# A fused attention and expert block with a deeper ring of gelus and a new hand-written order of its turn

## The reference

```python
h = tok(x); h = concat([h, txt], axis=1)                 # (64, 193, 128)
h = h + attn(layernorm(h))
h = h + ffn(layernorm(h))

# attn: 8 heads of 16; q and k have 8 features each, v has 16
qkv = group_norm(x @ W_qkv)                              # 32 groups, over tokens and features
logits = q k^T + q . rpe_k[i - j] + k . rpe_q[i - j]     # relative positions
attn = softmax(logits)
out = attn v + attn . rpe_v[i - j]
return group_norm(out)

# ffn: 8 experts of 512 hidden features, all of them computed, with the two top gate probabilities
for i in range(2):
    w_in = x * top_p[i]                                  # normalised to sum 1
    h = gelu(w_in @ W1 + b1)                             # exact gelu
    out += h @ W2 (summed over the experts) + sum(b2)
```

## Time and profile before

| | |
|---|---|
| median of 3 runs | 3409.49 us (3407.18 to 3465.08) |
| profiled execution | 3410.88 us, span 3409.1 us |
| mean granted TensorE clock | 0.987 |
| busy | PE 3132.8 us (92%), PEld 2577.5, ACT 1912.9 (56%), DVE 1897.9 (56%), POOL 1421.7 (42%) |
| first stage, start and the turn with attention alone | up to about 345 us |
| then | turns of 97.8 us |

### The profile page before, as it was taken

One profiled execution on the slowest core, in us unless ns is written; L12 is line 12 of the kernel. 1 busy time (PEld: TensorE's weight loads), 2 busy tenths in 40 slices (PEclk: granted clock), 3 DMA queues, 4 the chain that ended last, 5 costly groups with the idle time before them and its releaser, 6 DMA issues.

```text
span 3409.1 us, 62207 instructions
## 1 busy us (share of the span) xinstructions
PE 3132.8 (92%) x20032; PEld 2577.5 (76%) x20032; DVE 1897.9 (56%) x4113; ACT 1912.9 (56%) x4370; POOL 1421.7 (42%) x1350
## 2 busy tenths in 40 slices
PE   6977999999999999999999999999999999999998
PEld 5866778777777777777777777777777777777776
DVE  4644555555555555555555555555555555555554
ACT  4632555665555556655555566555555665555556
POOL 1001444454434444544344454444444544444446
PEclk9987999999999999999999999999999999999999
DMA  9951110111111001111110011111100111111010
GB/s 203 221 168 42 25 26 5 26 26 25 25 24 26 22 9 26 26 25 25 24 26 16 15 26 26 24 26 24 26 9 22 26 26 24 26 24 26 4 23 5
DMA packets 92173, 121.51 MB, mean 36 GB/s; under 512 B 8414, under 2 KB 86558, under 8 KB 87710
## 3 DMA queue, kind: packets, MB, share of 16 engines
q1 hardware_dynamic: 87714, 118.24, 14.9%
q10 hardware_dynamic: 4432, 2.93, 0.4%
HBM read 106.17 MB, written 14.97 MB: 36 GB/s over the span
## 4 chain that ended last, share of the span: by engine, by line
PE 54%; POOL 15%; issue 15%; DVE 5%; ACT 3%; POOLq 0%; DMA 0%; ACTq 0%; SPq 0%; DVEq 0%
POOL gelu L892 14%; PE bank L518 8%; PE bank L519 8%; PE bank L421 7%; PE bank L563 5%; PE bank L564 5%; PE bank L531 5%; PE bank L545 3%; PE bank L430 3%; PE bank L434 2%; PE bank L431 2%; PE bank L573 2%; PE bank L494 1%; PE bank L462 1%; ACT gelu L819 1%
## 5 line engine op out<-in xcount | busy, mean ns | idle before, releaser
L892 POOL TENSOR_TENSOR gelu<-gelu 128x386 f32<-128x386 f32 x1024 | 1040.3, 1031 | 1034.9 <-ACT gelu L820 1034.6
L819 ACT ACTIVATE gelu<-bank,b_s 128x386 f32<-128x386 f32 x1024 | 596.1, 582 | 805.2 <-DVE gelu L609 783.5
L421 PE MATMUL bank<-gelu,w_s 128*128 128x386 f32 x2048 | 842.0, 498 | 82.7 <-POOL gelu L892 82.7
L609 DVE TENSOR_TENSOR gelu<-bank,ratio 128x386 f32<-128x386 f32 x1024 | 565.8, 556 | 518.0 <-PE bank L434 514.6
L820 ACT ACTIVATE gelu<-gelu,b_s 128x386 f32<-128x386 f32 x1024 | 623.9, 609 | 0.0
L430 PE MATMUL bank<-x_hi,w_hi 128*128 128x386 f32 x1024 | 555.3, 542 | 73.5 <-ACT gelu L819 69.2
L421 PEld LDWEIGHTS bank<-gelu,w_s 128*128 128x128 f32 x2048 | 366.3, 191 | 149.5 <-POOL gelu L892 132.9
L860 ACT ACTIVATE lp<-bank,mx 128x193 f32<-128x193 f32 x800 | 328.9, 418 | 170.6 <-DVE mx L712 170.2
L518 PE MATMUL bank<-k_f,q_bd 128*128 128x193 f32 x1600 | 396.7, 330 | 8.4 <-DVE a_bd L702 8.4
L519 PE MATMUL bank<-rw,a_bd 128*128 128x193 f32 x1600 | 393.8, 328 | 0.0
L430 PEld LDWEIGHTS bank<-x_hi,w_hi 128*128 128x128 f32 x1024 | 194.7, 190 | 239.5 <-ACT gelu L819 140.3
(11 more groups left out here) (132 smaller groups left out, 4343.6 us busy)
## 6 DMA issues: line engine op xcount, KB each, us to landing
a_rep<-u_scratch SPq DMA_DIRECT2D x32, 1600.0 KB, 9.8
xt<-in_x SPq DMA_DIRECT2D x192, 196.0 KB
txt_s<-in_txt SPq DMA_DIRECT2D x32, 128.0 KB, 2.1
u_scratch<-k_f SPq DMA_DIRECT2D x32, 100.0 KB, 2.2
u_scratch<-q_f SPq DMA_DIRECT2D x32, 100.0 KB, 2.2
out<-o_s SPq DMA_DIRECT2D x64, 48.5 KB
out<-o_s SPq DMA_DIRECT2D x64, 48.0 KB
rv<-in_rel_v SPq DMA_DIRECT2D x1, 2624.0 KB, 14.6
```

The lines of the kernel that those rows point to most:

```text
L421: mm(yb[:, 0:T2], w2_s[:, f, :], gelu1[:, f % RING, :], start=(f == 0), stop=(f == NF - 1)).then_inc(S["w2_done"], 1)
L609: v.tensor_tensor(gelu2[:, f % RING, :], zb[f % 2][:, 0:T2], ratio[:, :], ALU.mult).then_inc(S["z2_done"], 1)
L819: a(gelu1[:, f % RING, :], zb[f % 2][:, 0:T2], ACT.Gelu, bias=b1_s[:, f:f + 1]).then_inc(S["g_done"], 1)
L892: g.tensor_tensor(gelu1[:, f % RING, :], gelu1[:, f % RING, :], gelu2[:, f % RING, :], ALU.add).then_inc(S["hs_done"], 1)
```

## The change

The ring has eight slots instead of four, and W2 runs four steps behind W1 instead of three; so there are four w2t at the end of a turn, and the first W2 of a pair comes with its fifth W1. The semaphores hs_done and w2_done start at RING, so that the waits for a slot need no special case. The norm copies of gaff on ACT are two steps of their own, nqk (q and k) and nv (v), and ACT's part of oaff is the step onorm. And the string has a new order. The work is the same.

```diff
-RING = 4
-LAG = 3
+RING = 8
+LAG = 4
-EARLY = "txt mean1 var1 bc1 proj gmean gvar gaff".split()
+EARLY = "txt mean1 var1 bc1 proj gmean gvar gaff nqk nv".split()
 SCHEDULE = (
-    "c c c am0 c qs0 c c vt hkeep log0 am1 log1 qs1 log2 am2 log3 qs2 log4 log5 am3 log6 qs3 log7 txt log8 "
-    "qs4 log9 mean1 log10 log11 var1 log12 tr0 tr1 bc1 rel0 c tr2 inv rel1 c tr3 rel2 tr4 rel3 tr5 rel4 tr6 rel5 rel6 "
-    "proj c pv0 c rec0 gmean pv1 c rec1 gvar place0 c place1 gaff c c omean c ovar c c oaff c oh2 c mean2 c var2 c c "
-    "bc2 c gate c c gate2 c c c c bcast w2t xin w2t w2t ot a otr a ocopy hres a"
+    "c qs0 vt am0 qs1 c c hkeep log0 am1 am2 log1 log2 txt log3 log4 mean1 log5 am3 log6 log7 log8 qs2 log9 log10 qs3 log11 qs4 log12 c var1 c tr0 c c inv tr1 rel0 tr2 rel1 tr3 rel2 tr4 bc1 rel3 c tr5 rel4 tr6 c rel5 rel6 proj pv0 gmean rec0 pv1 rec1 gvar place0 place1 c omean c gaff ovar c c c c c nqk c c oaff c onorm c oh2 c c mean2 nv c c var2 c c bc2 c gate gate2 c c bcast w2t w2t xin w2t w2t ot a a otr hres a ocopy"
...
         def ring_wait(eng, sem_, f, n):
-            if f >= RING or not is_first(n):
-                eng.wait_ge(sem_, n * NF + f - RING + 1)
+            eng.wait_ge(sem_, n * NF + f + 1)
...
-                pe.wait_ge(S["hs_done"], n * NF + f + 1)
+                pe.wait_ge(S["hs_done"], n * NF + f + 1 + RING)
...
-                    dve.wait_ge(S["w2_done"], n * NF + NF)
+                    dve.wait_ge(S["w2_done"], n * NF + NF + RING)
...
+            dve.sem_inc(S["hs_done"], RING)
+            dve.sem_inc(S["w2_done"], RING)
...
-                if s == "gaff":
+                sc, bi = gst[:, 5, :], gst[:, 6, :]
+                if s == "nqk":
                     act.wait_ge(S["affine"], t + 1)
-                    sc, bi = gst[:, 5, :], gst[:, 6, :]
                     for k, dst in enumerate((q_f, k_f)):
                         a(dst[:, 0:L], misc[:, 256 * k:256 * k + L], ACT.Identity,
                           bias=bi[:, k:k + 1], scale=sc[:, k:k + 1]).then_inc(S["norm"], 1)
+                elif s == "nv":
                     for b in range(2):
                         a(e2[:, b * L:(b + 1) * L], lg[0][:, b * L:(b + 1) * L], ACT.Identity,
                           bias=bi[:, 2 + b:3 + b], scale=sc[:, 2 + b:3 + b]).then_inc(S["norm"], 1)
...
-                elif s == "oaff":
+                elif s == "onorm":
                     act.wait_ge(S["oaffine"], t + 1)
```

## The result

The changed kernel took 3210.81 us (median of 4 runs, 3208.32 to 3213.52), beside 3408.34 us for the kernel before: a ratio of 0.9422, interval 0.9404 to 0.9441. The forecast was 3225 us, its range 3163 to 3315. The gain is 197.5 us, 6.4 us for each of the 31 turns.

A forecast was written before the change was run, and what follows sets the result against it. PE bounds each 97.80 us turn, with waits costing 9.5 us; remaining terms of 2.7, times 1.28, make 3.5, so 6.0 us gained over 31 turns: 3410.9 − 186 = 3225 us, range 3163 to 3315 (8 in 10).

The forecast's parts named there:

- Lag: At W2: the extra step removes five waits for POOL's sums, saving 4.05 us per turn; 0.15 remains at the last W2.
- Norm copies: W1 behind ACT's norm copies: loss falls from 1.83 to 0.35 us per turn, the v copies costing nothing.
- onorm and mean2: Output norm: two steps cover mean2's 1.34 us wait for oh2; onorm on ACT delays a W1 by 0.47 us.
- Start of the turn: Four W1 without a W2 instead of three: third to fifth W1 late by 0.53, 0.46 and 0.11, together 1.1 us.
- the factor 1.28: On the summed remaining waits: allowance for error in the step-by-step timing, raising 2.7 to 3.5 us per turn.
- Gate: Before the broadcast: gate2 follows gate with no product between, a 2.5 us chain; PE waits about 0.4 us.
- Attention part: Attention steps: moved products cover the transposes' wait; the remainder falls from 1.0 to 0.2 us per turn.
- SP: a_rep's load after later q/k copies: lands at t + 24, needed at t + 36.7; no wait, 12.7 us to spare.
- rival C: am0 holds DVE and every product until a_rep lands; slower, 3480 us in all; chance 0.04.
- Rival A: gaff, oaff, am0 and x_lo on DVE each wait for a POOL instruction: 2.9 us per turn, 3315 us; chance 0.15.
- Rival B: At the gate, POOL reaches the pow three sums behind; DVE and broadcast wait 2.9 us, 3315 us; chance 0.08.
- Rival D: W2's waits are ended by ACT's pace, not POOL's order: 4.05 us stay, 3350 us; no separate chance given.

The follow-up runs named there:

- e_new_small: The changed kernel's new step order with four slots and W2 three steps behind W1, instead of eight and four: 3331.7 us, ratio 0.9772.
- e_r8l3: The changed kernel with its eight slots and new order, but W2 three steps behind W1 instead of four: 3333.7 us, ratio 0.9781.
- e_joined: The changed kernel with the four norm copies together again, right behind gaff: 3250.1 us, ratio 0.9536.
- e_split_old: The kernel before with only the norm copies taken apart, q and k behind omean, v behind mean2: 3367.8 us, ratio 0.988.
- e_better2: The changed kernel with POOL's first two q spreads in the turn before, mean1 one logit later, a product between gate and gate2: 3158.0 us.
- e_ring_old: The kernel before, in its old order, with eight slots and W2 four steps behind W1: 3322.0 us, ratio 0.9747.
- e_gate: The changed kernel with one product moved from before nqk to between gate and gate2: 3187.3 us, ratio 0.9349.
- e_short_q: The changed kernel with POOL's q spreads 2 to 4 cut to one octet each from the second pair on: 3198.0 us, ratio 0.9384.

## Why the prediction was right

Step by step, with what the trace of the change shows:

- **Lag, 4.05 us saved, 0.15 left.** W2 waits 0.0 us. e_new_small and e_r8l3 show that it is the lag, not the slots. "The eight slots add no wait" holds, and they are worth 9 us. Alone in the old order the lag brought 2.8 us, since half a microsecond reappeared at mean2 and more at the gelus: the term holds only with the steps that clear those places. That the parts don't add is also in 87 + 77 (new order with lag three) = 164 against 197.
- **Norm copies, 1.83 to 0.35.** The W1 that waits behind nqk ends 0.31 us late, nv costs nothing. The count said that 1.5 us would be saved, and the place where the wait stood saved 1.5. The runs that change the copies alone give 1.3 per turn, but of e_joined's 1.3 only 0.6 is at the copies, and e_split_old leaves 0.78 there: the 0.35 holds for q and k behind the seventh product, not for any split.
- **onorm and mean2, 1.34 to 0.47.** mean2 doesn't wait in the turns; the delayed W1 is 0.38 late.
- **Start of the turn, 1.1.** The third, fourth and fifth W1 end 0.57, 0.45 and 0.12 us late: 1.14. The walk had 0.53, 0.46 and 0.11. So the factor 1.28, which I put on the sum because the same walk came out low on the old order, was not needed here. On the old order the walk was further off than it seemed: three W1s are late there, not two, by 0.37, 0.80 and 0.47 us, 1.64 in all (the first, at 1704.92, has no bracket).
- **Gate, 0.4.** It is 0.85 (0.57 idle, the rest restart). The size is off because L764 took 1.01 us in the turn, not the 0.45 of before. Timeline of DVE, then of POOL:

```profile
1695.60 1.01 DVE L764 TENSOR_SCALAR dl<-ep 97x4 f32<-97x4 f32 x1 [1.13 <-POOL ep L926]
1696.64 0.18 DVE L766 RECIPROCAL ep<-dl 97x4 f32<-97x4 f32 x1
1696.81 1.03 DVE L605 TENSOR_TENSOR gelu<-bank,ratio 128x386 f32<-128x386 f32 x2
```

```profile
1694.55 1.02 POOL L926 TENSOR_TENSOR ep<-half,dl 97x4 f32<-97x4 f32 x1 [1.62 <-DVE dl L761]
1695.54 1.95 POOL L891 TENSOR_TENSOR gelu<-gelu 128x386 f32<-128x386 f32 x2
```

POOL ends the pow and starts the next sum at 1695.54; DVE's operation, free at 1695.60, ends with the sum. Before, two multiplications stood between and held the same operation (L768) until 1693.17, 0.63 us into the sum that began at 1692.54, so it took 0.45. The prediction took that 0.45 over to a place where nothing stands between.
- **Attention part, 0.2.** Here two waits were missed: mean1 0.76 and the first logits 0.36, 1.1 us. The prediction had am1 and am2 nowhere in its sum.
- **SP.** No wait of DVE for a_rep inside the turns, as counted; rival C had no part in it.

What is left adds up to 0.31 + 0.38 + 1.14 + 0.85 + 1.1 = 3.8 us, beside a forecast of 3.5. So the factor that I added for an error of the walk (0.8 us) stood, by luck, for two waits that the walk had left out and for the gate.

By that count alone the gain would have been below the forecast, and it was 14 us above. The term that was too small is the loss of the turn before, 9.5 us: by the ends of the matmuls its waits come to about 10.0, because two of them have no bracket and weren't among the ten that it counted. The output transposes and the first of the three W1s end 0.37 us late each, in the timeline of PE before:

```profile
1703.61 0.68 PE L444 MATMUL bank<-con,hres 128*97 128x128 f32 x4
...
1704.92 0.45 PE L430 MATMUL bank<-x_hi,w_hi 128*128 128x386 f32 x1
```

10.0 less 3.8 is 6.2 of the 6.4 us; the last 0.2 isn't placed. Two errors of opposite sign, one in what was lost before and one in what is left, thus cancelled in part, which is luck. The lower end of the range rested on a misreading: L430 at 0.54 in the mean against "0.34 undisturbed". In e_better2, with PE busy for 99.36 of 100 us, the same product (L426) still takes 524 ns in the mean, and the steps in a dense stretch show 0.64 at the full pace of 1.18 us; its record overlaps W2's, so there was little to win in it.

**Rival A, the port,** had the right mechanism and the wrong places. gaff and oaff, at which it priced 2.6 us, met an idle POOL. Not by much: in e_joined, where only the copies moved, oaff met a sum and gst_o took 926 ns in the mean. Grouped by form, over the whole span of the change:

```profile
L698 DVE TENSOR_TENSOR a_bd<-a_rep,con 128x768 f32<-128x768 f32 x96 | 147.4, 1561 | 0.0
...
L764 DVE TENSOR_SCALAR dl<-ep 97x4 f32<-97x4 f32 x32 | 31.5, 984 | 36.1 <-POOL ep L926 36.1
...
L776 DVE TENSOR_TENSOR x_lo<-t,x_hi 128x386 fp32r<-128x386 f32 x32 | 27.8, 868 | 3.9
...
L650 DVE TENSOR_TENSOR gst_o<-gst_o 128x2 f32<-128x2 f32 x32 | 5.9, 186 | 1.1
```

The gst_o operation fell from 789 to 186 ns, x_lo (868 ns in the mean) and L764 grew. am1 to am3 grew from 1202 to 1561 in the mean. **Rival B** did not come: one pow stands ahead of two sums, not behind three. **Rival D** falls by its own sign: the waits of W2, which it had stay at 4.05 us, are gone in the change and in e_ring_old, and in e_new_small and e_r8l3 they come back, ended by POOL's sums.

## What to carry to other kernels

In a schedule of in-order engines, count the slack of each hand-over in steps of the bound engine (here 3 × 1.18 − 2.8 = 0.7 us) and compare it with the longest time that the producing queue stands still for something else (here the 1.0 us pow and its wait): one more step of lag was worth 120 us of 3330 in the new order, the four further buffers 9 us. An instruction that waits for another engine's round trip belongs behind independent work of its own engine, not ahead of it (e_gate, 23.5 us). And a wait that is removed from a periodic turn uncovers the next: price a part by undoing it in the final order as well as by doing it alone in the old one, and look in the trace whether the price lies at the part: half of e_joined's did not. A wait whose bracket is gone may still be there: compare the ends of the matmuls (mean1 in e_short_q, 0.32 us).

## What the runs showed of the hardware

A small DVE operation can be as long as a POOL operation beside it: L764, four columns, took 1.01 us when a sum of two SBUF tiles had started 0.06 us before it, and am1 and am2 3.74 us together beside sums and q spreads, where twice am3's 0.95 would be 1.9. It goes both ways: POOL's q spread took 1.28 us at the shortest and 1.76 in the mean in the change. An operation that reads one input from PSUM, L605, took 542 to 563 ns in all 1024 cases, with POOL busy 49% of the turn. The Trainium skill (SBUF — State Buffer, section “SBUF: two separate sides”) describes a lock of that kind for a DVE operation with two SBUF inputs or in a 2-port mode; L764 has a single SBUF input, so by that rule it is the mode that locks, which no run here tells apart.
